# A store moved behind the next image's sums in SyncE's queue, and GpSimd adds eleven tiles instead of twelve

## The reference

```
g     = clip(bn1(conv1x1(y)), 0, 6)                    # 64 channels
theta = y[:32]
f     = softmax(softmax(theta^T theta, axis=keys'), axis=queries')   # 3136 x 3136
out   = f g, depthwise 3 x 3 convolution, bn2, + y
```

## Time and profile before

| | |
|---|---|
| median of 3 runs | 5719.85 us (5717.09 to 5720.54) |
| profiled execution | 5723.8 us, its span 5721.9 us |
| TensorE busy | 92% |
| ScalarE busy | 90% |
| GpSimd busy | 82% |
| VectorE busy | 78% |
| mean granted TensorE clock | 0.957 of full speed |

### The profile page before, as it was taken

One profiled execution on the slowest core, in us unless ns is written; L12 is line 12 of the kernel. 1 busy time (PEld: TensorE's weight loads), 2 busy tenths in 40 slices (PEclk: granted clock), 3 DMA queues, 4 the chain that ended last, 5 costly groups with the idle time before them and its releaser, 6 DMA issues.

```text
span 5721.9 us, 90179 instructions
## 1 busy us (share of the span) xinstructions
PE 5287.3 (92%) x32898; PEld 2681.3 (47%) x32898; DVE 4463.7 (78%) x8965; ACT 5129.3 (90%) x3029; POOL 4668.5 (82%) x1913
## 2 busy tenths in 40 slices
PE   8999969989989898989898989899898989898995
PEld 3444435445545454545454544445454545454442
DVE  7888858878878787878787878788787878787875
ACT  7888859989989898989898989899898989898984
POOL 5666635888988888888888889889888888888885
PEclk9999969999999999999999999999999999999997
DMA  7887742222222222222222222122222222222211
GB/s 149 159 164 162 150 81 53 54 48 51 42 44 58 58 58 58 58 58 58 58 58 54 60 52 51 46 49 43 51 58 58 58 58 58 58 58 58 58 35 35
DMA packets 231221, 382.47 MB, mean 67 GB/s; under 512 B 161981, under 2 KB 179582, under 8 KB 220542
## 3 DMA queue, kind: packets, MB, share of 16 engines
q1 hardware_dynamic: 230782, 376.70, 31.4%
HBM read 260.16 MB, written 103.56 MB: 64 GB/s over the span
## 4 chain that ended last, share of the span: by engine, by line
PE 40%; POOL 17%; issue 11%; SPq 7%; ACT 6%; DMA 4%; DVE 3%; POOLq 0%; DVEq 0%
PE at_AV L963 21%; PE at_S L932 12%; POOL at_OUTB L758 6%; PE at_AV L969 5%; POOL at_ZP L745 5%; POOL at_ZB L756 3%; ACT at_ring L781 3%; ACT at_ring L787 3%; SPq L653 2%; DMA zd<-at_ZACC 2%; DVE at_ring L836 2%; PE at_AV L959 1%; SPq L629 1%; DMA rzd<-at_ZC 1%; POOL at_OUTB L760 1%
## 5 line engine op out<-in xcount | busy, mean ns | idle before, releaser
L836 DVE TENSOR_SCALAR_CACHE_REDUCE at_ring<-at_S 128x1176 f32<-128x1176 f32 (+1 forms) x2352 | 2889.8, 1242 | 322.1 <-PE at_S L932 294.2
L745 POOL TENSOR_TENSOR at_ZP<-at_ZP,at_ring 128x1568 f32<-128x1568 f32 x704 | 2505.1, 3601 | 381.9 <-ACT at_ring L787 350.5
L781 ACT ACTIVATE at_ring<-at_ring,at_NM 128x3136 f32<-128x3136 f32 x784 | 2278.0, 2906 | 380.3 <-DVE at_NM L845 375.0
L963 PE MATMUL at_AV<-at_ring,at_GT 128*64 128x392 f32 x12800 | 2352.3, 508 | 46.3 <-issue 39.5
L787 ACT ACTIVATE at_ring<-at_ring,at_RZ 128x3136 f32<-128x3136 f32 x784 | 2274.1, 2901 | 0.7 <-DVE at_RZ L853 0.7
L932 PE MATMUL at_S<-at_THM,at_THS 128*128 128x392 f32 x6144 | 1492.7, 371 | 307.9 <-DVE at_ring L836 264.3
L932 PEld LDWEIGHTS at_S<-at_THM,at_THS 128*128 128x128 f32 x6144 | 1043.7, 192 | 994.9 <-DVE at_ring L836 716.4
L963 PEld LDWEIGHTS at_AV<-at_ring,at_GT 128*64 128x64 f32 x12800 | 875.2, 139 | 1180.9 <-issue 1093.3
L758 POOL TENSOR_TENSOR at_OUTB<-at_OUTB,at_ZB 128x1568 f32<-128x1568 f32 x248 | 885.7, 3572 | 16.9
L969 PE MATMUL at_AV<-at_ring,at_ones 128*32 128x392 f32 x6656 | 618.5, 498 | 0.0
L458 DVE TENSOR_TENSOR l_U<-l_TY,l_XB 128x448 f32<-128x448 f32 x896 | 497.0, 617 | 99.4 <-PE l_TY L498 99.2
(11 more groups left out here) (70 smaller groups left out, 2520.5 us busy)
## 6 DMA issues: line engine op xcount, KB each, us to landing
l_X<-in_x SPq DMA_DIRECT2D x128, 392.0 KB, 7.5
at_THM<-hld SPq DMA_DIRECT2D x128, 392.0 KB, 7.5
at_THS<-hld SPq DMA_DIRECT2D x256, 192.0 KB, 4.3
at_CIN<-att SPq DMA_DIRECT2D x64, 406.0 KB, 7.6
at_ZB<-rzd SPq DMA_DIRECT2D x64, 406.0 KB, 4.9
yd<-l_YO SPq DMA_DIRECT2D x128, 196.0 KB, 5.5
att<-at_ACC SPq DMA_DIRECT2D x256, 98.0 KB
at_OUTB<-yd SPq DMA_DIRECT2D x64, 392.0 KB, 8.9
```

Of the source, the lines that this page charges most:

```text
L745: e.tensor_tensor(z, z, v, ALU.add).then_inc(g_add, 1)
L781: e.activation(v, v, ACT.Exp, bias=NM[:, i:i + 1], accum_out=ZS[:, i:i + 1]).then_inc(a_p1, 1)
L836: e.tensor_scalar(ring[:, s % RING, QC * a_:QC * b].rearrange("p (b w) -> p b w", w=QC), PS[:, k % 2, 0:b - a_, 0:QC], 1.0, None, ALU.mult ...
L963: ins = e.matmul(dst[64 * j:64 * j + 64, 0:QC], GT[fl.n % 2][:, keys_of(fl.n, t), :], ring[:, slot, q:q + QC], start=(t == GROUPS[fl.i][0] ...
```

## The change

In `POOL_OF` the entry of group 5 goes from 2 to 1: GpSimd adds eleven tiles of each image instead of twelve, and TensorE takes tile 20 itself in the "z" fills of group 5. The planner makes its orders anew with that. And the store of image n gets another due time in SyncE's list: no longer 15 steps behind the end of image n, but 3.9 steps behind the end of image n + 1, which is behind acc_out and z_in of image n + 1 and just ahead of z_out of image n + 1 (due at 4). The last image's store stays.

```diff
-POOL_OF = (2, 2, 2, 2, 2, 2, 0)
+POOL_OF = (2, 2, 2, 2, 2, 1, 0)
...
                 r = ready_at(n)
                 todo.append((r + 1.5, z_in, (n,)))
                 todo.append((r + 4, z_out, (n,)))
-                todo.append((r + 15, store, (n,)))
+                todo.append((ready_at(n + 1) + 3.9 if n + 1 < n_img else r + 15, store, (n,)))
```

## The result

The changed kernel takes 5471.45 us (median of 3 runs, 5470.96 to 5473.35) against 5719.85: a ratio of 0.9568, 95% interval 0.9546 to 0.9589, or 248 us less. The forecast was 5505, with 5450 to 5595 as its range.

The account below looks back on a forecast made before the run. It took TensorE and ScalarE as nearly full, both stopped by VectorE's wait for zd. Gains of 224 + 22 for the store and 14 at the end, less 45 for the tile, made 215 us: 5505 us, range 5450 to 5595.

Parts of the forecast that it names:

- What bounds the kernel: Middle of the run: TensorE and ScalarE nearly full, both stopped by VectorE's wait at L890 for zd, 283.3 us in all.
- no stretch in the middle with a clock under 0.95: Sign expected in the profile after: TensorE's granted clock stays at 0.95 or more throughout the middle.
- The store moved: SyncE's hold ahead of the sums goes: 14 long waits give 16 us each, 224; 15 short ones 1.5 each, 22.
- some 2.1 us are: VectorE's wait for zd at L890 left after the 3.3 us gap, with 4.1 us for landing; priced at 1.5 us.
- first rival: Sums land within 2 us of issue, so no wait at L890 is left: 21 us more gain, 5484 us; 7%.
- The store's own cost: Store ahead of z_out: 1.1 us to issue, 4.2 to land; L752 31.5 us behind the last addition; costed at nothing.
- This frees 7.2 us of an engine that isn't the bound, and gives nothing by itself: GpSimd's two additions fewer per image, 3.6 us each, were put at no gain on their own.
- I charge all of it: TensorE's extra tile in group 5 is paid in full: 31 images by 1.46 us, 45 us.
- The end: Last image: z_out waits for the store alone, 6.5 us less, and the convolution ends 7.2 earlier: 14 us gained.
- The second: Rival: TensorE takes the extra tile up in its free 1%, so the 45 us aren't paid: 5460 us; 10%.
- the fifth: Rival: SyncE is held as long at another place ahead of the sums: 5720 to 5765 us; 6%.
- The third and fourth: Rivals: GpSimd's ZP comes late and TensorE stands, 5595 us, 10%; the store closes a ring, 5813 us, 5%.

Follow-up runs that it names:

- e4: The changed kernel with ten GpSimd tiles instead of eleven, TensorE also taking one tile in group 4: 5453.0 us, ratio 0.9535.
- f2: The changed kernel with the tile that TensorE takes itself in group 4 instead of group 5, still eleven for GpSimd: 5458.0 us, ratio 0.9543.
- e1: The changed kernel with GpSimd keeping twelve tiles, so only the store is moved: 5442.0 us, ratio 0.9516.
- e2: The changed kernel with the store at its old place, so only the eleven tiles are new: 5474.8 us, ratio 0.9573.

## Why the prediction came out right, and where it was wrong

**What bounds the kernel.** Right that ScalarE and TensorE are nearly full and that VectorE's wait for zd stops both. That TensorE pays in full for whatever it gets was wrong: e4 and f2 show it. The sign "no stretch in the middle with a clock under 0.95" was wrong too: the low stretch in each pair is there without any wait of VectorE for zd, and costs 26.6 us in all.

**The store moved.** The sum had 224 + 22 and 14 for the end, of which 7.2 came from the tile on GpSimd; 253 us for the store alone. e1 measured 278. The mechanism is shown: no wait for zd is left in e1 or in the change. The size was off by 25 us, and the step that was mis-sized is the one that said "some 2.1 us are" left. It took 4.1 us for the landing, priced 14 waits at 1.5, 21 us. The landing took 0.9 us, because the move also took the loads out from ahead of the sums. The prediction's first rival, which says that nothing is left of the wait, had 7%. By the distances of L781, e1 has 262 us less in the fourteen middle pairs, where 224 and 21 of the 22 were put: 17 of the 25 us lie there. The other 8 lie in the last pair of images and behind it. One reading was wrong without weight: the store that SyncE issues at 3087.66 in the kernel before is that of image 13, for whose convolution it had waited, and not of image 12.

**The store's own cost.** The wait before z_out is 126.3 us in 31 times, 4.1 each, as put. L752 came at 2865.89, 26.5 us behind the end of the last addition (2839.37), where 31.5 had been put: 3.3 of the difference is the landing again, and 1.6 a shorter way from z_out to L752 (18.3 us against 19.9). It costs nothing, as put; TensorE never waits for ZP.

**Eleven tiles.** Two steps failed. "This frees 7.2 us of an engine that isn't the bound, and gives nothing by itself" holds only with the store moved: e2 shows 245 us for it alone. GpSimd wasn't full over the span, but it was full in the stretch that held SyncE. And "I charge all of it", 45 us, measured 29.5, which doesn't follow the tile's length: 9 us of it lie in the four steps where the clock falls (26.6 against 17.5 in e1).

**The end.** It comes 4.4 us earlier behind L760 (5415.12 to 5469.6, 54.5 us, against 58.9), not 6.5. In the chain of the changed kernel the last image's sums (zd landed at 5421.06) and not the convolution (done at 5418.69) set the store's issue at 5421.42.

**How the errors stand.** Store 25 us too little, tile 15.5 too much, and 7.2 for GpSimd's two additions at the end that weren't on the chain: 215 + 25 + 15.5 - 7.2 = 248, the measured value. That this closes proves nothing, since 29.5 is itself the difference of two of these runs. The halves don't add up in the other order: the 2 x 2 of before, e1, e2 and the change is 0, 278, 245 and 248.

**Rivals.** The second (the tile is free) is out as put, as is the fifth. The third and fourth didn't happen with eleven or twelve tiles; with thirteen TensorE waited at L969 in a part of the run.

What stays open is what decides whether TensorE's clock falls in a pair, why the loads ahead delay a sum's landing as much as they do, and why each bunching of fills costs what it does: this would need the fills' order moved one at a time.

## What to carry to other kernels

An in-order queue that waits for an engine puts that engine on the critical chain, however idle its share of busy time looks; look for what is queued behind the wait, and expect that relieving the engine and moving the wait are two ways to the same gain and not two gains. The time from issue to landing of a small transfer belongs to what was issued ahead of it: read it where the queue is as it will be after the change. Where an engine with a fixed step sets the pace, price added work on another engine by the steps that it makes longer, not by its length, look at the granted clock in the same steps, and give a planner's order more than one try.

## What the runs showed that I had not expected

The last transfer of 1.5 KB out of SyncE's queue landed 0.9 us behind the end of its issue where no large load had just gone out, and 1.9, 4.1 or 8.4 us where THM and half of THS (eight transfers, 4 x 392 and 4 x 192 KB) had been issued some 11, 9 or 1 us earlier. GpSimd at 1465.95 of 1500 us busy delivered all its sums in time, while in the same run, in pairs with another order, TensorE waited for it up to 15.8 us. And adding 512 matmul records to the change made the kernel faster, because TensorE's granted clock then stayed at 1.00 in a stretch where it had fallen in every pair.
